# Attention output by values as the stationary operand: y comes out already turned

## The chip, the cores and the metric

The kernel runs on one core of one Trainium2 chip. The metric is the device time of one execution in microseconds (us); of several executions the median counts. TensorE (PE) multiplies and transposes, VectorE (DVE), ScalarE (ACT) and GpSimd (POOL) do elementwise work, SyncE (SP) starts transfers. SBUF is the on-chip memory, PSUM the small one into which PE writes and which POOL can't read.

## The reference

A residual stream x of 2 x 2048 tokens by 256 channels passes three parts, the first and the last of one form, with a layer norm ahead of each:

```python
x = x + 0.5 * ffn(layernorm(x))
x = x + attention(layernorm(x))
x = x + 0.5 * ffn(layernorm(x))
```

`ffn` has a shared expert of width 2048 (silu(x sg) * (x su) sd) and eight routed experts of width 1024, two per token, with a capacity. The change lies in the attention, which works on groups of 64 tokens and 16 heads of 16 channels:

```python
qkv = einsum("bglc,cd->bgld", xg, w_qkv)       # q, k: rmsnorm times ln_w
att = softmax(causal(q @ k.T / 4))             # 64 x 64 per group and head
y = att @ v
out = y.reshape(B, T, 256) @ w_proj
```

## The kernel before

Everything is float32. PE multiplies in the type float32r, so each factor is split into a high part (rounded, made by ACT) and a low part (the rest, made by DVE or POOL), and a product is three products: high by high, high by low, low by high (`split_product`, L349).

The program is one list of instructions per engine, in an order written by hand; engines wait for each other by semaphores. Its phases are: the first ffn's shared part (half of it), its experts, the **fused stage**, then the rest of the second ffn. In the fused stage (`fused_step` on each engine, 40 steps) a step runs two chunks of the shared expert (gate, up, down products of 512 tokens) and between them, for the attention, one stage each of five different tiles of 128 tokens (two groups): `stats` (layer norm), `z` (q, k, v), `keys` (scores), `probs` (softmax and values) and `out` (projection). Eight chunks make a block, so c, the chunk at which a step begins, is 0, 2, 4 or 6; with c = 0 the down product of the chunk before comes early on PE, right behind the gate product.

On PE a step with all five stages is: gate(n); two transposes of y (`y_transpose`, L505); eight transposes of the exponentials p_s (`prob_transposes`, L538); `project` (L511); q, k, v (`qkv`, L516); up(n); the down product of the chunk before; gate(n+1); transposes of q and k (`head_transposes`); `scores` (L549); up(n+1); `values` (L566); down(n); two transposes of the next tile's normed rows (`z_transpose`).

The values: ph and pl are the high and low parts of the transposed exponentials of a pair of heads, 128 keys (two groups of 64) by 128 queries. They are the stationary operand (L576, L577), vv, the v of two heads with a high and a low half, is the moving one, and y comes out as tokens by channels, in two partial columns (from v high and v low) that DVE adds up (`outputs`, L1187: a reduction per half of the rows) and multiplies by the inverse sums rden:

```python
pe.matmul(quad[:, j // 4, o:o + P], ph[:, j, :], vv[:, q, j, :, :].rearrange("p a c -> p (a c)"), start=True, stop=False)
last = pe.matmul(quad[:, j // 4, o:o + 64], pl[:, j, :], vv[:, q, j, 0, :], start=False, stop=True)
```

In the next step PE turns y_s (its channels have to lie on the partitions for the projection), ACT copies the high part yh out of PSUM (L790) and DVE forms the low part yl = y - yh, with y read from PSUM (L1225).

The row sums of the softmax are made by POOL in two halvings (`row_halves`, L1427: half_s, quarter_s), which start when ACT has written the exponentials p_s (L824); DVE adds the last 16 columns (`row_sums`, L1200) and takes the reciprocal of 16 sums a token (`inverse_sums`, L1205). In a step with c other than 0, DVE's order is: yl, stats, the addition of the projection to x, pl (L1250), qke, row sums, reciprocal, the h product (L1044), the normed q and k (L1164), the low part of v (L1156), azn, hl, qkl, the masked scores (L1179), the row maximum, the h product of n+1, the outputs, azl, hl. `scores` on PE waits for the low part of v, since it overwrites v's PSUM bank; `values` waits for the masked scores for the same reason.

Of the kernel before, what the change touches and what calls it, by code (L numbers as in the profile page):

```python
# [28 lines left out]
def program(nc, x_in, w_qkv, ln_w, w_proj, router_w, rg, ru, rd, sg, su, sd, out):  # L29
# [33 lines left out]
    with ExitStack() as ctx:  # L63
# [9 lines left out]
        def sem(name):  # L73
# [88 lines left out]
        vv = sb("vv", [P, VDEEP, NH // 2, 2, 64], F32R, att)  # L162
# [9 lines left out]
        rden = sb("rden", [P, NH], F32, att)  # L172
        y_s = sb("y_s", [P, C], F32, att)
# [3 lines left out]
        quarter_s = sb("quarter_s", [P, NH, GROUP // 4], F32, att)  # L177
# [24 lines left out]
            a_exp a_pt a_ph a_pl a_vh a_vl a_y a_yn a_yt a_yh a_yl a_o a_x a_pad a_const a_qkt a_qkh a_qkl  # L202
            qkh_sv0 qkh_sv1 qkl_sv0 qkl_sv1 heads_in0 heads_in1 a_masked a_ysum a_max a_rden a_den a_half a_quarter pool_const""".split()
# [127 lines left out]
        def wait_hl(eng, n):  # L331
            if in_fused(n):
                eng.wait_ge(sm["hl_fused"], n - FUSED[0] + 1)
            else:
                eng.wait_ge(sm["hl_done"], n + 1 - (FUSED[1] - FUSED[0] if n >= FUSED[1] else 0))

# [11 lines left out]
        def _(pe):  # L348
# [147 lines left out]
            def z_transpose(t, uses):  # L496
                pe.wait_ge(sm["a_zn"], t + 1)
                wait(pe, sm["a_pl"], t - 2)
# [39 lines left out]
            def prob_transposes(t, z, uses):  # L538
                pe.wait_ge(sm["a_exp"], t + 1)
                pe.wait_ge(sm["a_qkl"], z if z is not None else NT)  # L540
                pe.wait_ge(sm["a_zl"], z + 1 if z is not None else NT)
                if uses:
                    pe.wait_ge(sm["misc_free"], max(uses) + 1)
# [22 lines left out]
            def values(t, z, keys, out):  # L566
# [17 lines left out]
            def fused_step(s):  # L584
# [11 lines left out]
                if out is not None:  # L596
                    y_transpose(out)
# [4 lines left out]
                if probs is not None and keys is not None:  # L602
                    prob_transposes(probs, z, uses)
                if out is not None:
                    project(out)
                if z is not None:
                    qkv(z, out)
                up(n, b % 2, c, buf, SB)
# [6 lines left out]
                if keys is not None and probs is not None:  # L615
                    scores(keys, z, out)
                up(n + 1, b % 2, c + 1, buf, SB)
                if keys is not None and probs is None:
                    scores(keys, z, out)
                if any(block_at(pf, step, pb, c) is not None for step in ("T", "R", "M")):  # L620
                    wait(pe, sm["a_pl"], probs + 1 if probs is not None else upto(s, -LAG["probs"]))
# [7 lines left out]
                assert all(block_at(pf, step, pb, c + 1) is None for step in ("T", "R", "M"))  # L629
                if ahead is not None:  # L630
# [51 lines left out]
        def _(act):  # L682
# [89 lines left out]
            def values_high(t):  # L772
                act.wait_ge(sm["a_v"], t + 1)
                wait(act, sm["a_y"], t + 1 - VDEEP)
                for g in range(2):
                    for r in range(2):
                        src = quad[64 * g:64 * g + 64, 1, 0:C].rearrange("p (j r d) -> p j r d", r=2, d=HD)[:, :, r, :]
                        o = 32 * g + HD * r
                        last = nc.scalar.copy(vv[64 * r:64 * r + 64, t % VDEEP, :, 0, o:o + HD], src)
                last.then_inc(sm["a_vh"], 1)  # L780

            def fused_step(s):
# [4 lines left out]
                if out is not None:  # L787
                    act.wait_ge(sm["a_yt"], out + 1)
                    wait(act, sm["a_x"], out)
                    nc.scalar.copy(yh[:, :, :], chunks(quad[:, 1, 0:C])).then_inc(sm["a_yh"], 1)  # L790
# [13 lines left out]
                heads_first = z is not None and (c == 0 or out is None)  # L804
# [5 lines left out]
                if heads_first:  # L810
                    h_high(n, SB)
                prep(pf, pb, c)
# [42 lines left out]
        def _(dve):  # L855
# [292 lines left out]
            def values_low(t, groups=(0, 1)):  # L1148
                dve.wait_ge(sm["a_vh"], t + 1)
                q = t % VDEEP  # L1150
                for g in groups:
                    for r in range(2):
# [3 lines left out]
                        last = v.tensor_tensor(vv[rows, q, :, 1, o:o + HD], src, vv[rows, q, :, 0, o:o + HD], ALU.subtract)  # L1156
# [30 lines left out]
            def outputs(t):  # L1187
                dve.wait_ge(sm["a_y"], t + 1)
                wait(dve, sm["a_yt"], t)
# [4 lines left out]
                last.then_inc(sm["a_ysum"], 1)  # L1194
                dve.wait_ge(sm["a_rden"], t + 1)
                dve.wait_ge(sm["a_ysum"], t + 1)
                y_heads = y_s[:, :].rearrange("p (h d) -> p h d", d=HD)
                v.tensor_tensor(y_heads, y_heads, rden[:, :].unsqueeze(2).broadcast_to([P, NH, HD]), ALU.mult).then_inc(sm["a_yn"], 1)

            def row_sums(t):  # L1200
                dve.wait_ge(sm["a_quarter"], t + 1)
                wait(dve, sm["a_rden"], t)
                v.tensor_reduce(den_a[:, :], quarter_s[:, :, :], AX, ALU.add).then_inc(sm["a_den"], 1)

            def inverse_sums(t):  # L1205
                dve.wait_ge(sm["a_den"], t + 1)
                wait(dve, sm["a_yn"], t)
                v.reciprocal(rden[:, :], den_a[:, :]).then_inc(sm["a_rden"], 1)
# [10 lines left out]
            def fused_step(s):  # L1219
# [21 lines left out]
                if drained:  # L1241
                    h_product(n, SB)
                if s:
# [4 lines left out]
                if probs is not None:  # L1248
                    dve.wait_ge(sm["a_ph"], probs + 1)
# [530 lines left out]
```

## Time and profile before

| | |
|---|---|
| median of 3 runs | 2122.65 us (2120.07 to 2126.28) |
| the profiled execution | 2113.96 us |
| its span, first to last instruction | 2112.2 us |
| mean granted clock of TensorE | 0.996 of 2.4 GHz |
| busy: PE, DVE, ACT, POOL | 99%, 64%, 46%, 23% of the span |
| values products of the fused stage (L576), first and last start | 732.2 and 1269.3 us after the span's start |

The span is the time between the profile's first and last instruction; the execution's own time is 1.8 us longer. A busy PE is not PE at its peak: the ends of matmuls are modelled, and starts are the better measure of what one costs.

### The profile page before, as it was taken

The page shows a single profiled execution, that of the slowest core. Times are in us where ns is not written, and L with a number is a line of the kernel's source. Part 1 is how long each engine was busy: PE and PEld are TensorE (multiplying, and loading weights), DVE is VectorE, ACT ScalarE, POOL GpSimd, SP SyncE. Part 2 cuts the span into 40 slices and gives each one's busy share as a digit, 9 for nine tenths or more (in the row PEclk, how much of TensorE's full clock was granted, in tenths as well). Part 3 has the DMA queues.
Part 4 walks back from the last instruction along what each step waited for, and adds up shares of the span by engine and source line. Part 5 has one row for each costly group of instructions (what it writes and reads, how often), then busy time and mean ns, then how long its engine had stood idle before and what let it go on. Part 6 is the DMA issues. An engine that isn't in the chain of part 4 may idle for free.

```text
span 2112.2 us, 37639 instructions
## 1 busy us (share of the span) xinstructions
PE 2082.5 (99%) x13844; PEld 1912.4 (91%) x13844; DVE 1360.0 (64%) x3108; ACT 962.3 (46%) x1910; POOL 493.1 (23%) x433
## 2 busy tenths in 40 slices
PE   9999999999999999999999999999999999999999
PEld 7888899999998788888887888888999999988888
DVE  7666556666665688888888876665566666633333
ACT  3333335555553565655665542333455555523232
POOL 2423211121212233223334433322021211200000
PEclk9999999999999999999999999999999999999999
DMA  9331225554436344444455432221244444531010
GB/s 275 104 115 59 76 64 132 134 141 113 106 86 198 81 118 112 111 118 98 113 116 131 121 109 75 79 90 48 82 106 111 103 102 104 125 115 60 30 61 21
DMA packets 295976, 218.70 MB, mean 104 GB/s; under 512 B 69241, under 2 KB 276525, under 8 KB 295792
## 3 DMA queue, kind: packets, MB, share of 16 engines
q1 hardware_dynamic: 278128, 194.92, 32.9%
q0 software_dynamic: 17664, 21.38, 5.7%
q8 instruction: 110, 1.80, 0.4%
q14 instruction: 74, 0.61, 0.1%
HBM read 129.48 MB, written 93.23 MB: 105 GB/s over the span
## 4 chain that ended last, share of the span: by engine, by line
PE 89%; DVE 6%; issue 2%; ACT 1%; DMA 1%; SPq 1%; POOL 0%; DVEq 0%; ACTq 0%
PE gate_up_p L353 29%; PE quad L353 25%; PE out_p L391 22%; PE misc L391 4%; PE quad L576 2%; PE quad L561 2%; PE misc L545 1%; PE quad L577 1%; PE misc L417 1%; DVE h_s L1044 1%; PE misc L428 1%; PE misc L426 1%; PE misc L409 1%; DMA stage<-in_L_ffn_rd 1%; DVE p_s L1179 1%
## 5 line engine op out<-in xcount | busy, mean ns | idle before, releaser
L353 PE MATMUL gate_up_p<-zh,w 128*128 128x512 f32 (+2 forms) x2368 | 703.1, 359 | 2.0 <-DVE h_s L1044 1.4
L731 ACT CAST hh<-h_s 128x512 fp32r<-128x512 f32 (+2 forms) x511 | 276.2, 541 | 671.1 <-DVE h_s L1044 654.3
L353 PE MATMUL quad<-zh,w 128*128 128x512 f32 (+2 forms) x1728 | 481.7, 346 | 0.0
L353 PEld LDWEIGHTS gate_up_p<-zh,w 128*128 128x128 f32 x2368 | 429.9, 189 | 49.8 <-DVE h_s L1044 2.4
L391 PE MATMUL out_p<-w,hh 128*128 128x256 f32 x2808 | 458.8, 282 | 6.6 <-DVE hl L1128 5.2
L391 PEld LDWEIGHTS out_p<-w,hh 128*128 128x128 f32 x2808 | 403.8, 189 | 28.9 <-DVE hl L1128 9.0
L353 PE MATMUL gate_up_p<-zl,w 128*128 128x512 f32 (+2 forms) x1184 | 421.4, 356 | 0.0
L1044 DVE TENSOR_TENSOR h_s<-gate_up_p,sg_s 128x512 f32<-128x512 f32 (+2 forms) x296 | 178.4, 603 | 246.6 <-PE gate_up_p L353 244.6
L1060 DVE TENSOR_TENSOR hl<-h_s,hh 128x512 fp32r<-128x512 f32 (+2 forms) x431 | 247.1, 573 | 136.4 <-ACT hh L731 120.9
L353 PEld LDWEIGHTS quad<-zh,w 128*128 128x128 f32 x1728 | 308.5, 188 | 24.6
L353 PE MATMUL quad<-zl,w 128*128 128x512 f32 (+2 forms) x864 | 295.4, 342 | 0.0
L1496 POOL DMA_INDIRECT y_d<-eo,tmeta x80 | 128.8, 1611 | 617.7 <-DVE eo L943 590.2
L720 ACT ACTIVATE sg_s<-gate_up_p 128x512 f32<-128x512 f32 (+2 forms) x296 | 156.6, 529 | 212.2 <-PE gate_up_p L353 210.7
L1044 DVE TENSOR_TENSOR h_s<-quad,sg_s 128x512 f32<-128x512 f32 (+2 forms) x215 | 122.9, 572 | 200.6 <-PE quad L353 172.6
L353 PEld LDWEIGHTS gate_up_p<-zl,w 128*128 128x128 f32 x1184 | 223.5, 189 | 19.9
L391 PE MATMUL out_p<-w,hl 128*128 128x256 f32 x1404 | 225.2, 279 | 0.0
L391 PEld LDWEIGHTS out_p<-w,hl 128*128 128x128 f32 x1404 | 192.7, 189 | 0.0
L1473 POOL DMA_INDIRECT slots_d<-zn,slot_i x128 | 129.2, 1010 | 187.9 <-DVE zn L1037 143.6
L353 PEld LDWEIGHTS quad<-zl,w 128*128 128x128 f32 x864 | 162.7, 188 | 11.4
L720 ACT ACTIVATE sg_s<-quad 128x512 f32<-128x512 f32 (+2 forms) x216 | 108.7, 503 | 114.3 <-PE quad L353 113.3
L714 ACT CAST w<-stage 128x384 fp32r<-128x384 f32 x256 | 131.1, 512 | 25.7 <-DMA stage<-in_L_ffn_rd 21.9
L966 DVE TENSOR_TENSOR w<-stage,w 128x384 fp32r<-128x384 f32 x256 | 140.5, 549 | 0.0
(189 smaller groups left out, 2532.8 us busy)
## 6 DMA issues: line engine op xcount, KB each, us to landing
stage<-in_L_ffn_rg SPq DMA_DIRECT2D x128, 128.0 KB, 2.8
stage<-in_L_ffn_ru SPq DMA_DIRECT2D x128, 128.0 KB, 3.0
stage<-in_L_ffn_rd SPq DMA_DIRECT2D x128, 128.0 KB, 3.2
heads_d<-qkh SPq DMA_DIRECT2D x128, 128.0 KB
q_t<-heads_d SPq DMA_DIRECT2D x32, 384.0 KB, 4.6
k_t<-heads_d SPq DMA_DIRECT2D x64, 192.0 KB, 4.8
slots_d<-empty SPq DMA_DIRECT2D x16, 662.5 KB, 7.4
zh_d<-zh SPq DMA_DIRECT2D x16, 512.0 KB, 3.2
```

Of the source, the lines that this page charges most:

```text
L353: last = pe.matmul(dst, a, b, start=(k == 0), stop=(k == 3 * n - 1))
L391: last = pe.matmul(out[:, j // 2, o:o + C], a[:, par, cols], w[:, hi, :], start=(c == 0 and i == 0 and j % 2 == 0), stop=(c == NCH - 1 and ...
L561: last = pe.matmul(quad[0:rows, j // 4, o:o + P].rearrange("p (r c) -> p r c", r=2), queries[:, at:at + rows], k_t[:, j, :, own], start=(g ...
L576: pe.matmul(quad[:, j // 4, o:o + P], ph[:, j, :], vv[:, q, j, :, :].rearrange("p a c -> p (a c)"), start=True, stop=False)
L714: nc.scalar.copy(W[buf_of(f, u)][:, 0, j, o:o + HALF_PIECE], stage[:, j % 2, o:o + HALF_PIECE]).then_inc(sm["wh_done" if o else "wh_half"], 1)
L720: nc.scalar.activation(sg_s[:, n % 2, 0:ncol], gate_p[bank_of(n)][:, 0:ncol], ACT.Silu).then_inc(sm["silu_done"], 1)
L731: nc.scalar.copy(hh[:, n % 2, 0:ncol], h_s[:, n % 2, 0:ncol]).then_inc(sm["hh_done"], 1)
L966: last = v.tensor_tensor(w[:, 1, j, cols], stage[:, j % 2, cols], w[:, 0, j, cols], ALU.subtract)
L1044: v.tensor_tensor(h_s[:, n % 2, 0:ncol], up_p[bank_of(n)][:, 0:ncol], sg_s[:, n % 2, 0:ncol], ALU.mult).then_inc(sm["h_done"], 1)
L1060: v.tensor_tensor(hl[:, n % 2, 0:ncol], h_s[:, n % 2, 0:ncol], hh[:, n % 2, 0:ncol], ALU.subtract).then_inc(sm["hl_done"], 1)
L1473: g.indirect_dma_start(out=slots_d[f], out_offset=bass.IndirectOffsetOnAxis(ap=slot_i[:, c, t:t + 1], axis=0), in_=zn[:, k % 2, j, :], in_ ...
L1496: g.indirect_dma_start(out=y_d[f], out_offset=bass.IndirectOffsetOnAxis(ap=tmeta[:, q, j:j + 1], axis=0), in_=eo[:, par, j, :], in_offset= ...
```

## The change

The roles in the values product are exchanged. Per head pair there are now three products with 66 columns of v as the stationary operand (64 are used: two groups by two heads by 16 channels) and ph or pl as the moving one: v high by p high, v high by p low, v low by p high. y comes out with channels on the partitions and tokens along the row, as the projection needs it. So:

- the two transposes of y on PE go; the inverse sums, which lie with tokens on the partitions, are turned instead: the reciprocal writes each of the 16 values of a token 16 times (rden is 128 x 256), PE transposes it twice behind the scores (`inverse_transposes`), and ACT copies the result to rdt in SBUF;
- `outputs` on DVE is now eight products of 32 partitions by 128 elements, each picking a group's own quarter of PSUM and multiplying it by rdt; no reduction is left;
- yh and yl are formed from y_s in SBUF;
- vv has one flat row of 16 x 64 + 4 columns; quarter_s goes, the second halving writes into half_s;
- row sums and reciprocal stand in front of the low part of v in all steps (behind qkl with c = 0 before), and the drained steps at the end have an order of their own;
- POOL subtracts the low part of the weight pieces (four steps only) before its softmax subtraction, no longer behind it.

```diff
-        vv = sb("vv", [P, VDEEP, NH // 2, 2, 64], F32R, att)
+        vv = sb("vv", [P, VDEEP, NH * 64 + 4], F32R, att)
...
-        rden = sb("rden", [P, NH], F32, att)
+        rden = sb("rden", [P, NH, HD], F32, att)
+        rdt = sb("rdt", [P, KC, P], F32, att)
...
-            def y_transpose(t):
-                pe.wait_ge(sm["a_yn"], t + 1)
+            def inverse_transposes(t):
+                pe.wait_ge(sm["a_rden"], t + 1)
+                pe.wait_ge(sm["a_pl"], t + 1)
                 for k in range(KC):
-                    last = pe.transpose(quad[:, 1, k * P:(k + 1) * P], y_s[:, k * P:(k + 1) * P], ident[:, :])
-                last.then_inc(sm["a_yt"], 1)
+                    o = C + k * P
+                    last = pe.transpose(misc[:, 1, o:o + P], rden[:, NH // KC * k:NH // KC * (k + 1), :].rearrange("p h d -> p (h d)"), ident[:, :])
+                last.then_inc(sm["a_rt"], 1)
...
-                    pe.matmul(quad[:, j // 4, o:o + P], ph[:, j, :], vv[:, q, j, :, :].rearrange("p a c -> p (a c)"), start=True, stop=False)
-                    last = pe.matmul(quad[:, j // 4, o:o + 64], pl[:, j, :], vv[:, q, j, 0, :], start=False, stop=True)
+                    dst = quad[0:GROUP + 2, j // 4, o:o + P]
+                    vh, vl = (vv[:, q, (2 * j + a) * 64:(2 * j + a) * 64 + GROUP + 2] for a in range(2))
+                    pe.matmul(dst, vh, ph[:, j, :], start=True, stop=False)
+                    pe.matmul(dst, vh, pl[:, j, :], start=False, stop=False)
+                    last = pe.matmul(dst, vl, ph[:, j, :], start=False, stop=True)
...
-                    nc.scalar.copy(yh[:, :, :], chunks(quad[:, 1, 0:C])).then_inc(sm["a_yh"], 1)
+                    nc.scalar.copy(yh[:, :, :], y_s[:, :, :]).then_inc(sm["a_yh"], 1)
...
+                if probs is not None:
+                    act.wait_ge(sm["a_rt"], probs + 1)
+                    wait(act, sm["a_yn"], probs)
+                    nc.scalar.copy(rdt[:, :, :], chunks(misc[:, 1, C:2 * C])).then_inc(sm["a_rr"], 1)
...
-                yp = quad[:, :, :].rearrange("p b (j a c) -> p (b j) c a", a=2, c=64)
                 for g in range(2):
-                    rows = slice(64 * g, 64 * g + 64)
-                    last = v.tensor_reduce(y_s[rows, :].rearrange("p (j c) -> p j c", c=2 * HD), yp[rows, :, 32 * g:32 * g + 32, :], AX, ALU.add)
...
-                v.tensor_tensor(y_heads, y_heads, rden[:, :].unsqueeze(2).broadcast_to([P, NH, HD]), ALU.mult).then_inc(sm["a_yn"], 1)
+                    tokens = slice(GROUP * g, GROUP * g + GROUP)
+                    for m in range(4):
+                        rows = slice(32 * m, 32 * m + 32)
+                        own = quad[32 * g:32 * g + 32, :, m * P + GROUP * g:m * P + GROUP * g + GROUP]
+                        last = v.tensor_tensor(y_s[rows, :, tokens], own, rdt[rows, :, tokens], ALU.mult)
+                last.then_inc(sm["a_yn"], 1)
...
-                v.reciprocal(rden[:, :], den_a[:, :]).then_inc(sm["a_rden"], 1)
+                v.reciprocal(rden[:, :, :], den_a[:, :].unsqueeze(2).broadcast_to([P, NH, HD])).then_inc(sm["a_rden"], 1)
...
-                    v.tensor_tensor(yl[:, :, :], chunks(quad[:, 1, 0:C]), yh[:, :, :], ALU.subtract).then_inc(sm["a_yl"], 1)
+                    v.tensor_tensor(yl[:, :, :], y_s[:, :, :], yh[:, :, :], ALU.subtract).then_inc(sm["a_yl"], 1)
...
-                if probs is not None and c:
+                if probs is not None and not drained:
                     row_sums(probs)
                     inverse_sums(probs)
...
+                if 0 <= refill(s) < NCH:
+                    pool.wait_ge(sm["a_qkl"], z + 1)
+                    piece_low(refill(s))
                 if keys is not None:
                     pool.wait_ge(sm["a_max"], keys + 1)
                     g.tensor_tensor(p_s[:, :, :], p_s[:, :, :],
                                     smax[:, :].unsqueeze(2).broadcast_to([P, NH, GROUP]), ALU.subtract).then_inc(sm["a_sub"], 1)
-                if 0 <= refill(s) < NCH:
-                    piece_low(refill(s))
-
```

How the instructions stand, at three places. The first is PE, from the last scores product to the values; before:

```order
L561 MATMUL quad<-k_t,q_t 66x128
L353 MATMUL gate_up_p<-zh,w 128x512
L353 MATMUL gate_up_p<-zl,w 128x512
L353 MATMUL gate_up_p<-zh,w 128x512 x2
L353 MATMUL gate_up_p<-zl,w 128x512
L353 MATMUL gate_up_p<-zh,w 128x512
L576 MATMUL quad<-vv,ph 128x128
L577 MATMUL quad<-vv,pl 128x64
```

And now (L567 the scores, L513 the inverse sums' transposes, L356 the up product, L584 to L586 the values):

```order
L567 MATMUL quad<-k_t,q_t 66x128
L513 MATMUL misc<-ident,rden 128x128 x2
L356 MATMUL gate_up_p<-zh,w 128x512
L356 MATMUL gate_up_p<-zl,w 128x512
L356 MATMUL gate_up_p<-zh,w 128x512 x2
L356 MATMUL gate_up_p<-zl,w 128x512
L356 MATMUL gate_up_p<-zh,w 128x512
L584 MATMUL quad<-ph,vv 66x128
L585 MATMUL quad<-pl,vv 66x128
L586 MATMUL quad<-ph,vv 66x128
```

Two transposes have come between scores and up product, and a pair of values products has become three, with an output of 66 rows.

The second is DVE in a step with c = 0, from qke to the masked scores; before:

```order
L1254 TENSOR_SCALAR qke<-ssq 128x2
L1156 TENSOR_TENSOR vv<-quad,vv 64x8x16 x2
L1164 SCALAR_TENSOR_TENSOR qk<-quad,qkr,lnw 128x256 x2
L1156 TENSOR_TENSOR vv<-quad,vv 64x8x16 x2
L1044 TENSOR_TENSOR h_s<-gate_up_p,sg_s 128x512
L1146 TENSOR_SCALAR azn<-x,amv,ard 128x256
L1172 TENSOR_TENSOR qkl<-misc,qkh 128x512
L1203 TENSOR_REDUCE den_a<-quarter_s 128x16
L1208 RECIPROCAL rden<-den_a 128x16
L1179 TENSOR_TENSOR p_s<-quad,causal 128x1024
```

And now:

```order
L1279 TENSOR_SCALAR qke<-ssq 128x2
L1221 TENSOR_REDUCE den_a<-half_s 128x16
L1226 RECIPROCAL rden<-den_a 128x256
L1171 TENSOR_TENSOR vv<-quad,vv 64x8x16 x2
L1179 SCALAR_TENSOR_TENSOR qk<-quad,qkr,lnw 128x256 x2
L1171 TENSOR_TENSOR vv<-quad,vv 64x8x16 x2
L1059 TENSOR_TENSOR h_s<-gate_up_p,sg_s 128x512
L1161 TENSOR_SCALAR azn<-x,amv,ard 128x256
L1187 TENSOR_TENSOR qkl<-misc,qkh 128x512
```

Row sums and reciprocal have moved from behind qkl to in front of vv, and the reciprocal has grown from 16 to 256 columns.

The third is DVE from the outputs to yl, at the seam of two steps; before:

```order
L1193 TENSOR_REDUCE y_s<-quad 64x256 x2
L1198 TENSOR_TENSOR y_s<-y_s,rden 128x256
L1293 TENSOR_TENSOR azl<-misc,azh 128x256
L1128 TENSOR_TENSOR hl<-h_s,hh 128x512
L1225 TENSOR_TENSOR yl<-quad,yh 128x256
```

And now:

```order
L1211 TENSOR_TENSOR y_s<-quad,rdt 32x2x64 x8
L1315 TENSOR_TENSOR azl<-misc,azh 128x256
L1143 TENSOR_TENSOR hl<-h_s,hh 128x512
L1243 TENSOR_TENSOR yl<-y_s,yh 128x256
L948 SCALAR_TENSOR_TENSOR x<-out_p,x 128x1024
```

Two reductions and a multiplication have become eight small products, and yl reads y_s in place of quad.

## Rows read from the trace of the kernel before

**Rows 1.** The page's part 1: busy us (share of the span) and instructions.

```profile
PE 2082.5 (99%) x13844; PEld 1912.4 (91%) x13844; DVE 1360.0 (64%) x3108; ACT 962.3 (46%) x1910; POOL 493.1 (23%) x433
```

**Rows 2.** Waits of PE from 732 to 1266 us: total, times, longest.

```profile
PE quad L576 <- DVE p_s L1179: 3.3, 8, 1.3
```

**Rows 3.** PE's timeline in a step with c = 2: start us, us, instruction.

```profile
884.56 0.72 PE L391 MATMUL out_p<-w,hh 128*128 128x256 f32 x4
...
887.63 0.38 PE L508 MATMUL quad<-ident,y_s 128*128 128x128 f32 x2
887.85 1.07 PE L545 MATMUL misc<-ident,p_s 128*128 128x128 f32 x8
888.93 0.50 PE L353 MATMUL quad<-aw,yh 128*128 128x256 f32 x2
...
896.35 1.58 PE L561 MATMUL quad<-k_t,q_t 96*128 96x128 f32 x16
897.76 0.44 PE L353 MATMUL gate_up_p<-zh,w 128*128 128x512 f32 x1
...
899.24 0.33 PE L576 MATMUL quad<-vv,ph 128*128 128x128 f32 x1
...
901.05 0.72 PE L391 MATMUL out_p<-w,hh 128*128 128x256 f32 x4
```

**Rows 4.** PE's timeline in the step before it, c = 0.

```profile
867.39 0.71 PE L391 MATMUL out_p<-w,hh 128*128 128x256 f32 x4
...
870.75 0.74 PE L391 MATMUL out_p<-w,hh 128*128 128x256 f32 x4
...
873.03 0.48 PE L353 MATMUL quad<-aw,yh 128*128 128x256 f32 x2
...
879.50 1.56 PE L561 MATMUL quad<-k_t,q_t 96*128 96x128 f32 x16
...
882.75 0.33 PE L576 MATMUL quad<-vv,ph 128*128 128x128 f32 x1 [0.24 <-DVE p_s L1179]
```

**Rows 5.** VectorE's timeline in these two steps.

```profile
876.30 0.17 DVE L1254 TENSOR_SCALAR qke<-ssq 128x2 f32<-128x2 f32 x1
877.25 0.58 DVE L1156 TENSOR_TENSOR vv<-quad,vv 64x128 fp32r<-64x128 f32 x2 [0.79 <-ACT vv L779]
...
888.46 0.42 DVE L1225 TENSOR_TENSOR yl<-quad,yh 128x256 fp32r<-128x256 f32 x1 [0.55 <-ACT yh L790]
...
891.27 1.23 DVE L1250 TENSOR_TENSOR pl<-misc,ph 128x1024 fp32r<-128x1024 f32 x1 [0.90 <-ACT ph L795]
...
892.93 0.25 DVE L1208 RECIPROCAL rden<-den_a 128x16 f32<-128x16 f32 x1
893.49 0.69 DVE L1044 TENSOR_TENSOR h_s<-gate_up_p,sg_s 128x512 f32<-128x512 f32 x1 [0.31 <-PE gate_up_p L353]
...
894.88 1.19 DVE L1156 TENSOR_TENSOR vv<-quad,vv 64x128 fp32r<-64x128 f32 x4
```

**Rows 6.** ScalarE's timeline in the step of rows 3.

```profile
886.71 1.06 ACT L824 ACTIVATE p_s<-p_s 128x1024 f32<-128x1024 f32 x1
888.05 0.37 ACT L790 CAST yh<-quad 128x256 fp32r<-128x256 f32 x1 [0.28 <-PE quad L508]
...
901.07 0.62 ACT L731 CAST hh<-h_s 128x512 fp32r<-128x512 f32 x1 [2.29 <-DVE h_s L1044]
```

**Rows 7.** Timeline of POOL and VectorE in a later step.

```profile
1165.94 1.28 POOL L1429 TENSOR_TENSOR half_s<-p_s 128x512 f32<-128x512 f32 x1 [0.61 <-ACT p_s L824]
1165.99 1.78 DVE L1128 TENSOR_TENSOR hl<-h_s,hh 128x512 fp32r<-128x512 f32 x1
```

**Rows 8.** VectorE's groups by shape, whole run: busy us, mean ns | idle before.

```profile
L1193 DVE TENSOR_REDUCE y_s<-quad 64x256 f32<-64x512 f32 x64 | 43.9, 687 | 10.6 <-PE quad L577 10.2
...
L1208 DVE RECIPROCAL rden<-den_a 128x16 f32<-128x16 f32 x32 | 8.1, 253 | 1.1
...
L890 DVE RECIPROCAL rec<-vare 128x4 f32<-128x4 f32 x15 | 2.7, 178 | 0.5
```

More of the change, by code:

```diff
@@ L335, in wait_hl, with vv_at @@
                 eng.wait_ge(sm["hl_done"], n + 1 - (FUSED[1] - FUSED[0] if n >= FUSED[1] else 0))
+        def vv_at(rows, q, part):
+            return vv[rows, q, 0:NH * 64].rearrange("p (j a c) -> p j a c", a=2, c=64)[:, :, part, :]
         def tile_at(s, stage):
@@ L601, in fused_step @@
                     down_of(*chunk_before(f, phase, b, c))
-                if probs is not None and keys is not None:
+                if out is not None and keys is not None:
                     prob_transposes(probs, z, uses)
@@ L607, in fused_step @@
                     qkv(z, out)
+                if probs is not None and out is None:
+                    prob_transposes(probs, z, uses)
                 up(n, b % 2, c, buf, SB)
@@ L616, in fused_step @@
                     scores(keys, z, out)
+                if probs is not None:
+                    inverse_transposes(probs)
                 up(n + 1, b % 2, c + 1, buf, SB)
-                if keys is not None and probs is None:
-                    scores(keys, z, out)
                 if any(block_at(pf, step, pb, c) is not None for step in ("T", "R", "M")):
-                    wait(pe, sm["a_pl"], probs + 1 if probs is not None else upto(s, -LAG["probs"]))
+                    wait(pe, sm["a_rr"], probs + 1 if probs is not None else upto(s, -LAG["probs"]))
                     wait(pe, sm["a_qkl"], upto(s, 1 - LAG["z"]))
@@ L629, in fused_step @@
                 assert all(block_at(pf, step, pb, c + 1) is None for step in ("T", "R", "M"))
+                if keys is not None and probs is None:
+                    scores(keys, z, out)
                 if ahead is not None:
@@ L803, in fused_step @@
                     values_high(z)
-                heads_first = z is not None and (c == 0 or out is None)
+                heads_first = z is not None and c == 0
                 if not heads_first:
@@ L1242, in fused_step @@
                     h_product(n, SB)
+                    if probs is not None:
+                        prob_low(probs)
+                    fused_low(n)
+                    if probs is not None:
+                        row_sums(probs)
+                        inverse_sums(probs)
+                    if keys is not None:
+                        masked(keys)
                 if s:
@@ L1254, in fused_step @@
                     v.tensor_scalar(qke[:, :], ssq[:, :], 1.0 / C, RMS_EPS, ALU.mult, ALU.add).then_inc(sm["a_qke"], 1)
-                if probs is not None and c:
+                if probs is not None and not drained:
                     row_sums(probs)
                     inverse_sums(probs)
-                heads_first = z is not None and (c == 0 or out is None)
+                heads_first = z is not None and c == 0
                 if not heads_first and not drained:
@@ L1270, in fused_step @@
                     normal(ahead)
-                if not heads_first:
+                if not heads_first and not drained:
                     fused_low(n)
@@ L1274, in fused_step @@
                     heads_low(z)
-                if probs is not None and not c:
-                    row_sums(probs)
-                    inverse_sums(probs)
                 if keys is not None and probs is None:
                     h_product(n + 1, SB)
-                if keys is not None:
+                if keys is not None and not drained:
                     masked(keys)
@@ L1436, in fused_step @@
                 f, phase, b, c = fused_chunk(s)
-                z, keys, probs, ahead = (tile_at(s, stage) for stage in ("z", "keys", "probs", "stats"))
+                z, keys, probs, out, ahead = (tile_at(s, stage) for stage in ("z", "keys", "probs", "out", "stats"))
                 n = chunk(f, phase, b, c)
```

43 lines of the change are left out of this document (20 added, 23 removed).

## The prediction

> **What bounds the kernel now.** I read the engines' busy time first: TensorE (PE) is busy for 2082.5 of the span's 2112.2 us [rows 1], so only what lengthens or shortens PE's own sequence, or makes PE wait, moves the end. The change touches no transfer, and of the work the fused stage alone (attention between shared-expert chunks, 32 token tiles in 40 steps). The list of waits, cut to the steps that hold values, shows how little PE waits there: its longest sum is 3.3 us in 8 waits, for the masked scores [rows 2]. Then I followed one step through the engines' timelines. I call V the moment when a step's last values product is issued and the down product behind it starts. Three steps in four (those in which c is 2, 4 or 6) run as [rows 3] do, from V = 884.56 to the next V at 901.05, 16.49 us; the step with c = 0 [rows 4] runs from 867.39 to 884.56, 17.17 us. All times below are us after V.
>
> What sets the pace in [rows 3] is nearly even. PE's probability transposes start at 3.29, 0.08 after ScalarE's exponential ends (886.71 + 1.06, 3.21) [rows 6]. The projection starts at 4.37, when VectorE has formed y's low part (3.90 + 0.42) [rows 5]. The scores start at 11.79, 0.28 after VectorE's last low part of v (894.88 + 1.19, 11.51) [rows 5]. VectorE is thus off the end only by some tenths of a us: the reader should see in [rows 5] that it waits just 0.31 before its h product, behind the reciprocal.
>
> **The change, part by part, in a step with c other than 0.**
>
> *Values on PE.* Now 16 products, each with a stationary operand 128 wide, take 1.81 (899.24 to 901.05), 0.113 each [rows 3]. They become 24 with a stationary operand 66 wide and 128 moving columns. The scores are eight of each width in 1.41 (896.35 to 897.76) [rows 3]; less 8 times 0.113, a 66-wide one costs 0.063. I take 24 x 0.063 = 1.51, a gain of 0.30. Bounds: 0.058 (0.113 x 66/128) and 0.113, that is 1.39 to 2.71. By the Trainium skill, "TensorE: Matmul & The Clock Gate", Back-to-back issue gap, a stream of loads and products of 128 columns holds about 81 ns each; by it the values would take an estimated 1.94, a loss of 0.13 in place of the gain. No row here shows 81 ns at that width.
>
> *Transposes.* The two of y leave the start of the step (0.22, 887.63 to 887.85 [rows 3]); but the probability transposes still need the exponential, so they start at about 3.27 as before. Two of the inverse sums enter between scores and up product; they cost 0.15 (bounds 0.13 and 0.22). They wait for the reciprocal, which ends long before the scores do, so the up product queued behind them is not held. ScalarE's copy of them (as yh, 0.37) falls into its idle time before hh, 2.29 [rows 6].
>
> *Outputs on VectorE.* Two reductions of 0.69 [rows 8] and a multiplication end 1.92 after they start. Now come eight products of 32 partitions by 128 elements. The nearest row is the low part of v, 64 x 128, four in 1.19 [rows 5], 0.30 each: 8 x 0.30 = 2.4, +0.5. Bounds 0.21 and 0.42 each (half and the whole of yl's 256 elements [rows 5]). Behind them azl and hl end at about 3.68 in place of 3.3.
>
> *y's low part.* It read PSUM and SBUF; now y_s and yh both lie in SBUF. [Rows 7] show what that means while GpSimd (POOL) adds the row halves: an SBUF-with-SBUF subtraction issued at 1165.99, just after POOL's 1.28, lasts 1.78: it ends 0.55 after POOL does. The old yl, of the same step place but from PSUM, is not held: 0.42, inside POOL's time [rows 5]. POOL starts at the exponential's end, and yh comes behind the exponential on ScalarE, so yl is always issued inside POOL's 1.28. With hl in front of it holding POOL up a little, POOL's 1.28 runs from about 3.5 to 4.75; yl has half the elements of the held row, so it ends 0.29 behind POOL, at 5.04, and the projection starts at 5.10 (0.05 after yl, as 888.93 is after 888.88): 0.73 later than now. The row sums that POOL also delays have 3 us to spare.
>
> *The reciprocal.* 16 elements become 256. Another operation on 256, yl, costs 0.42 [rows 5]; this one costs 178 ns on 4 and 253 on 16 [rows 8], 6.25 ns an element, so 0.253 + 240 x 0.00625 = 1.75. Bounds 0.42 (the rate of other rows) and 4.0 (16 rows of 16). I take the slope, since it comes from the operation itself. The Trainium skill, "VectorE: DVE Perf Modes", First, the fixed hardware budget, calls it an iterative divide repeated 8 times; at the 0.96 GHz of its Specifications that is 8.3 ns an element and an estimated 2.25 us, some 15 us more in all than the sum below. The rows show the lower slope.
>
> *The path.* Behind the projection come the q and k product and ScalarE's squares of it; VectorE's qke, which needs them, starts 3.27 after the projection (873.03 [rows 4] to 876.30 [rows 5]): 8.37. The row sums start 0.07 later and take 0.45, so the reciprocal starts at 8.89 and h at 8.89 + 1.67 = 10.56 (two operations in a row overlap by 0.08). Now h starts at 8.93 [rows 5]. From h to the scores VectorE's sequence is unchanged, 2.58 to the end of v's low part and 0.06 more: scores at 13.20. PE alone would be there at 5.10 + 7.42 (888.93 to 896.35 [rows 3]) = 12.52, so a new wait in front of the scores, for the low part of v, sets the step. Scores to values takes 2.89 + 0.15, the values 1.51: V at 17.75. **+1.26.**
>
> **The step with c = 0.** The down product that now starts at 3.36 (870.75 [rows 4]) needs hl, which ends at 3.68: +0.38. The collision of yl is covered by that product. Row sums and reciprocal come in front of the low part of v, where VectorE now waits 0.79 for ScalarE [rows 5]: qke starts at 8.91 + 0.38, the sums at 9.36, and the reciprocal ends at 11.48; v's low part, at 9.86 now, starts then. The scores come 2.25 after v's first low part (877.25 to 879.50 [rows 4, 5]), at 13.73, against 12.11. From scores to values it is 3.25, of which the wait of 0.24 for the masked scores [rows 4] goes, since the sums no longer stand in front of them; with 0.15 and 1.51, V comes at 18.40. **+1.23.**
>
> **The sum.** 15 steps x 1.26 = 18.9; 6 x 1.23 = 7.4; the eight later steps that also carry routing or weight pieces, where VectorE is fuller: 1.3 each, 10.4, less 4 for the weight pieces that POOL now subtracts before its softmax subtraction, clear of hl and yl ([rows 7] are such a case of crowding). First and drained steps: 0, within 2. Together +32.7 us. The profiled execution took 2113.96; the median of the three timed runs is 2122.65 (2120.07 to 2126.28), above it by 8.7. Against the median I forecast 2155; against the profiled execution it would be 2146. About 0.3% (6.4 us) is what a measurement of this kernel can tell from no change.
>
> **Rivals.**
> - *yl gets through before POOL* (its neighbour hl holds the access until just before). Then the projection starts behind the eight transposes, near 4.15. yh starts at 3.11 instead of 3.49, so pl comes at 6.33 instead of 6.71 [rows 5, 6], the reciprocal 1.66 later at 7.99, h at 9.66, V at 16.85: +0.36 in 15 steps, 5.4; 7.4; eight at 0.7 less 4, 1.6. +14, 2137. Against it: in [rows 7] the vector operation waits for POOL's end.
> - *The reciprocal costs 0.42*, as other 256-element rows, with yl held. Then h waits for up, 4.56 after the projection (888.93 to 893.49), 9.66; scores at 12.52, V at 17.07: +0.58 in 15 steps, 8.7; c = 0: 0; the rest 0. +9, 2132. Against it: the slope of its own two rows.
> - *The other side: VectorE's additions fit into its idle time and PE goes on setting the step.* Place: the stretch from yl to the h product. It decides where the reciprocal stays below about 0.8 us and yl is not held: then up bounds h (4.15 + 4.56), scores start at 4.15 + 7.42 less 0.1 of restart, V at 16.02, -0.47 in 15 steps, 7.0; c = 0: 0; the rest -6. -13, 2110. For it: PE's own sequence does get shorter by the values' 0.30. Against it: both rows named above.
> - *The narrow stationary operand saves nothing*: 0.113 each, values 2.71, which adds 1.20 in 29 steps to the forecast: 2190. Against it: the scores' rows.
>
> **How the numbers follow.** Forecast 0.50; yl free 0.15; cheap reciprocal 0.16; the other side 0.12; wide price 0.07. The cheap reciprocal lies at the bound, half of it counts as the same. Faster 0.12, same 0.08, slower 0.80. The forecast's own range is 2143 to 2168 (outputs, loaded steps). The range reaches down over two rivals and up for dearer outputs, leaving out the last two rivals: 2128 to 2170.
>
> **What would show it.** Right: a reciprocal near 1.75; yl near 1.3 to 1.5 instead of 0.42; PE's longest wait in the stage in front of the scores, for the low part of v, about 0.7 in three steps of four; values in 1.5; steps of 17.7 and 18.4. Wrong: a reciprocal below 0.8, or scores that start within 0.3 of the q and k transposes' end in steps that are not longer than 16.5.

## The result and the profile after

The changed kernel takes 2185.51 us, the median of 4 runs (2183.81 to 2187.58); the kernel before took 2121.38 beside it. The ratio is 1.0295, with a 95% interval of 1.0276 to 1.0314. The forecast was 2155, from 2128 to 2170: slower, as it said, but by 64 us in place of 33.

The two profiled executions lie 71.5 us apart in span (2183.7 against 2112.2). The page's part 1 after, against [rows 1]:

```profile
PE 2097.1 (96%) x14100; PEld 1914.0 (88%) x14100; DVE 1444.9 (66%) x3268; ACT 971.5 (44%) x1942; POOL 498.7 (23%) x433
```

VectorE (DVE) has 85 us more to do, and TensorE (PE) waits. The list of PE's waits from 700 to 1345 us (what is waited for: total, times, longest):

```profile
PE misc L540 <- DVE qk L1179: 22.5, 18, 3.1
PE quad L356 <- DVE yl L1243: 17.1, 21, 1.3
PE quad L567 <- DVE vv L1171: 10.8, 21, 0.5
PE out_p L394 <- DVE hl L1143: 8.4, 11, 3.5
PE misc L513 <- DVE rden L1226: 5.3, 2, 3.3
```

In the kernel before, the same stretch has for the first four of these places:

```profile
PE out_p L391 <- DVE hl L1128: 5.2, 4, 1.9
...
PE misc L535 <- DVE qk L1164: 2.4, 4, 1.2
PE quad L561 <- DVE vv L1156: 2.0, 4, 0.5
...
PE quad L353 <- DVE yl L1225: 1.5, 3, 0.8
```

The second and third after are the two that were forecast (y's low part, v's low part). The first, q and k transposes that wait for VectorE's normalized q and k, which stand behind the reciprocal, was not named in the forecast: 7.2 us of it lie in the regular steps (1.1 in each with c = 0), 11.7 behind them.

**Most regular steps with c not 0 are as forecast.** Nine of the 15 take 17.69 to 17.73 us (forecast 17.75). PE's timeline of one of them, with c = 4, from V = 925.72 to the next V at 943.41, 17.69 us (the step just before it, the one that answers to [rows 3], took 19.00 and comes further down):

```profile
925.72 0.68 PE L394 MATMUL out_p<-w,hh 128*128 128x256 f32 x4
...
928.98 1.06 PE L551 MATMUL misc<-ident,p_s 128*128 128x128 f32 x8
930.79 0.50 PE L356 MATMUL quad<-aw,yh 128*128 128x256 f32 x2 [0.74 <-DVE yl L1243]
...
938.90 1.57 PE L567 MATMUL quad<-k_t,q_t 96*128 96x128 f32 x16 [0.51 <-DVE vv L1171]
940.31 0.40 PE L513 MATMUL misc<-ident,rden 128*128 128x128 f32 x2
...
941.94 0.22 PE L584 MATMUL quad<-ph,vv 128*66 128x128 f32 x1
942.00 0.23 PE L585 MATMUL quad<-pl,vv 128*66 128x128 f32 x1
942.06 0.22 PE L586 MATMUL quad<-ph,vv 128*66 128x128 f32 x1
```

The projection starts at V + 5.07 (forecast 5.10), the scores at V + 13.18 (13.20), and the values follow each other at 0.06 us. VectorE and POOL in the same step, against [rows 5] and [rows 7]:

```profile
929.24 1.49 DVE L1243 TENSOR_TENSOR yl<-y_s,yh 128x256 fp32r<-128x256 f32 x1
...
934.04 0.17 DVE L1279 TENSOR_SCALAR qke<-ssq 128x2 f32<-128x2 f32 x1 [0.71 <-ACT qk L812]
934.12 0.42 DVE L1221 TENSOR_REDUCE den_a<-half_s 128x16 f32<-128x256 f32 x1
934.58 1.75 DVE L1226 RECIPROCAL rden<-den_a 128x256 f32<-128x256 f32 x1
936.24 0.63 DVE L1059 TENSOR_TENSOR h_s<-gate_up_p,sg_s 128x512 f32<-128x512 f32 x1
...
937.57 1.19 DVE L1171 TENSOR_TENSOR vv<-quad,vv 64x128 fp32r<-64x128 f32 x4
```

```profile
928.96 1.49 POOL L1452 TENSOR_TENSOR half_s<-p_s 128x512 f32<-128x512 f32 x1 [1.67 <-ACT p_s L839]
```

y's low part starts while POOL adds and ends 0.28 after it; the reciprocal takes 1.75; h starts at V + 10.52 (10.56).

**What was not forecast is elsewhere.** Measured between the starts of the down product behind the values, the two traces compare so (us in the profile of before, and what the others have more or less; the experiments' columns come into use below). The eight loaded steps carry routing or weight pieces besides what the regular ones do; the two drained ones, at the end, no longer have the q, k, v stage:

| | before | after | recip16 | yl_first | both | scalar_copy_filled |
|---|---|---|---|---|---|---|
| up to the first values' end | 734.0 | +9.7 | +4.7 | +8.0 | +4.5 | +0.1 |
| 15 regular steps, c not 0 | 247.4 | +23.0 | +12.1 | +7.5 | -4.5 | -5.0 |
| 6 regular steps, c = 0 | 103.1 | +8.6 | -1.2 | +10.2 | -1.1 | -1.6 |
| 8 loaded steps | 151.4 | +22.4 | +6.7 | +23.5 | +5.7 | -1.3 |
| 2 drained steps | 33.8 | +5.8 | +5.1 | +5.4 | +1.3 | -0.3 |
| the rest | 842.4 | +2.0 | +1.2 | +1.5 | +3.1 | +0.4 |
| span | 2112.2 | +71.5 | +28.5 | +56.1 | +9.1 | -7.7 |

The forecast had 18.9, 7.4, 6.4 and 0 for the lines from regular to loaded and the others together. And TensorE's granted clock fell: its mean is 0.986 after and 0.996 before. The windows of two equal steps with c = 0, one without and one with a fall, two stretches inside the latter, and a loaded step (from and to, length, busy us of PE, PEld, DVE, ACT, POOL with instructions, granted clock, DMA share, GB/s):

```profile
888.64:906.72 18.08, 16.46 (x126) 14.20 (x124) 16.93 (x34) 10.58 (x21) 5.12 (x5) 1.00 0.56 141
815.84:835.51 19.67, 18.05 (x126) 15.43 (x124) 17.73 (x34) 11.12 (x22) 6.45 (x6) 0.91 0.52 146
...
831.00:832.00 1.00, 1.00 (x6) 0.90 (x5) 0.83 (x1) 0.37 (x1) 0.00 (x0) 0.50 0.35 86
832.00:833.00 1.00, 1.00 (x4) 0.80 (x3) 1.00 (x3) 0.99 (x1) 0.00 (x0) 0.50 0.53 181
...
1190.35:1213.61 23.26, 19.78 (x127) 17.27 (x126) 18.71 (x45) 12.03 (x23) 10.83 (x9) 0.85 0.42 104
```

PE's work is the same 126 instructions, but takes 18.05 us in place of 16.46, since the clock stands at 0.50 (1.2 GHz) in stretches such as the two shown. Over the span 1 - 0.986 of 2183.7 is 30.6 us, against 8.4 before. By this estimate some 22 of the 71.5 us are clock, and 49 are work and waits; it counts PE as if it set the pace throughout the stretches at 0.50, so 22 is rather too much than too little. About 10 of the 22 lie in the loaded steps (granted clock 0.92 over their 173.8 us, 0.98 over the 151.4 before).

### The profile page after: what moved, and what is told of

It reads as the page before. It is cut to its first block, busy times and chain, and to the rows that moved or that the text cites. A ratio compares the mean times of both kernels' runs of the same rounds, so it can differ in the third digit from the quotient of the medians.

```text
span 2183.7 us, 38401 instructions
## 1 busy us (share of the span) xinstructions
PE 2097.1 (96%) x14100; PEld 1914.0 (88%) x14100; DVE 1444.9 (66%) x3268; ACT 971.5 (44%) x1942; POOL 498.7 (23%) x433
## 4 chain that ended last, share of the span: by engine, by line
PE 47%; DVE 15%; issue 5%; ACT 1%; DVEq 0%; POOL 0%; ACTq 0%; POOLq 0%
PE quad L356 15%; PE gate_up_p L356 14%; PE out_p L394 11%; DVE y_s L1211 3%; PE misc L394 2%; DVE hl L1143 2%; PE quad L567 2%; DVE h_s L1059 1%; DVE yl L1243 1%; DVE qk L1179 1%; DVE vv L1171 1%; DVE p_s L1194 1%; DVE rden L1226 1%; DVE pl L1216 1%; DVE den_a L1221 1%
## 5 line engine op out<-in xcount | busy, mean ns | idle before, releaser
L356 PE MATMUL gate_up_p<-zh,w 128*128 128x512 f32 (+2 forms) x2368 | 710.6, 362 | 1.0 <-DVE zl L1373 0.5
L356 PE MATMUL quad<-zh,w 128*128 128x512 f32 (+2 forms) x1728 | 481.8, 346 | 0.0
L356 PEld LDWEIGHTS gate_up_p<-zh,w 128*128 128x128 f32 x2368 | 433.2, 190 | 51.2 <-issue 1.9
L356 PE MATMUL gate_up_p<-zl,w 128*128 128x512 f32 (+2 forms) x1184 | 424.6, 359 | 0.2 <-issue 0.2
L356 PEld LDWEIGHTS quad<-zh,w 128*128 128x128 f32 x1728 | 308.5, 188 | 24.7
L356 PE MATMUL quad<-zl,w 128*128 128x512 f32 (+2 forms) x864 | 295.4, 342 | 0.0
L356 PEld LDWEIGHTS gate_up_p<-zl,w 128*128 128x128 f32 x1184 | 225.2, 190 | 19.8
L356 PEld LDWEIGHTS quad<-zl,w 128*128 128x128 f32 x864 | 162.7, 188 | 11.4
L725 ACT CAST w<-stage 128x384 fp32r<-128x384 f32 x256 | 131.1, 512 | 25.3 <-DMA stage<-in_L_ffn_rd 22.3
```

What stands on the lines that cost most here:

```text
L356: last = pe.matmul(dst, a, b, start=(k == 0), stop=(k == 3 * n - 1))
L725: nc.scalar.copy(W[buf_of(f, u)][:, 0, j, o:o + HALF_PIECE], stage[:, j % 2, o:o + HALF_PIECE]).then_inc(sm["wh_done" if o else "wh_half"], 1)
```

## Experiments

Theory A: the wide reciprocal and the held low part of y lengthen VectorE's chain, and the waits that they give PE also let its clock fall. Theory B: what exceeds the forecast comes from the moved orders in the filling steps (those ahead of the first values), the loaded and the drained ones. Each ratio below is to the kernel before as timed beside that run; its median went from 2116.02 to 2121.38 us, so differences between runs are given by the ratios too.

**recip16**: the reciprocal of 16 sums, then a copy 16 times wide.

```diff
+rd_a = sb("rd_a", [P, NH], F32, att)
...
-v.reciprocal(rden[:, :, :], den_a[:, :].unsqueeze(2).broadcast_to([P, NH, HD])).then_inc(sm["a_rden"], 1)
+v.reciprocal(rd_a[:, :], den_a[:, :]).then_inc(sm["a_ra"], 1)
+dve.wait_ge(sm["a_ra"], t + 1)
+v.tensor_copy(rden[:, :, :], rd_a[:, :].unsqueeze(2).broadcast_to([P, NH, HD])).then_inc(sm["a_rden"], 1)
```

> The changed kernel, but the reciprocal is taken of 16 sums and then copied 16 times wide by VectorE (about 0.25 + 0.35 us in place of 1.75). Theory A (the wide reciprocal and the held low part of y lengthen VectorE's chain, and TensorE's waits that follow also let its granted clock fall): every step loses about 1.1 us and most of the stretches at a granted clock of 0.5 go; 2130 to 2150 us. Theory B (the loss beyond the forecast comes from the moved orders, in the filling, loaded and drained steps): only the regular steps gain, 21 x 0.7 = 15 us; 2165 to 2175 us, mean clock still near 0.986.

Measured: 2142.48, ratio 1.0114 (1.0098 to 1.0131), mean clock 0.994. VectorE's groups (busy us, mean ns):

```profile
L1229 DVE COPY rden<-rd_a 128x256 f32<-128x256 f32 x32 | 9.4, 294 | 1.1
L1227 DVE RECIPROCAL rd_a<-den_a 128x16 f32<-128x16 f32 x32 | 8.1, 253 | 1.1
```

1753 ns have become 547 (253 + 294), and 43 us go (38 by the two ratios): theory A. The table has 10.9 of them in the regular steps with c not 0, 9.8 in those with c = 0, and 22.3 in the other lines.

**yl_first**: POOL's row halves wait until y's low part is formed.

```diff
 pool.wait_ge(sm["a_exp"], t + 1)
+wait(pool, sm["a_yl"], t)
```

> The changed kernel, but GpSimd's row halves wait until the low part of y is formed. Theory A: the low part of y takes 0.4 to 0.5 us in place of 1.26, the projection starts 0.8 us earlier, steps with c other than 0 get 0.7 us shorter, some falls of the clock go; 2155 to 2170 us. Theory B: 2180 to 2190 us, since other work is late by as much.

Measured: 2170.09, ratio 1.0246 (1.0229 to 1.0263). Timeline of a step with c not 0 (16.8 us long):

```profile
936.81 0.42 DVE L1243 TENSOR_TENSOR yl<-y_s,yh 128x256 fp32r<-128x256 f32 x1
937.36 1.28 POOL L1453 TENSOR_TENSOR half_s<-p_s 128x512 f32<-128x512 f32 x1 [2.53 <-ACT p_s L839]
```

The price of the collision is shown: 15 us between the two profiles (10 by the ratios), and the steps with c not 0 hold it (23.0 to 7.5). That some falls of the clock would go was wrong: the mean clock is 0.984, no higher than without the edit.

**both**: both edits.

> Both edits together (16-wide reciprocal with a copy; row halves behind the low part of y). Theory A: TensorE's own sequence sets most steps again, with the values 0.3 us shorter; 2110 to 2130 us, mean granted clock 0.993 or more. Theory B: 2145 to 2165 us, mean clock still near 0.986.

Measured: 2123.32, ratio 1.0018 (1.0004 to 1.0031), clock 0.993. So 59 of the 63 us (by the ratios) were these two prices together with the falls behind them, more than the 38 and 10 of the single edits added. Nine of the 15 regular steps with c not 0 now take 16.0 to 16.1 against 16.5: PE's timeline has no wait in them, and its sequence is shorter. Those with c = 2 take 16.3 to 16.4, and one takes 17.0.

**before_recip256**: the kernel before with the wide reciprocal, nothing else.

```diff
-rden = sb("rden", [P, NH], F32, att)
+rden = sb("rden", [P, NH, HD], F32, att)
...
-v.reciprocal(rden[:, :], den_a[:, :]).then_inc(sm["a_rden"], 1)
+v.reciprocal(rden[:, :, :], den_a[:, :].unsqueeze(2).broadcast_to([P, NH, HD])).then_inc(sm["a_rden"], 1)
```

> The kernel before, but its reciprocal writes all 256 elements (1.75 us in place of 0.25) and the product with y reads them; nothing else is changed. Theory A: the scores come 1.2 us later in 15 steps and in most loaded ones, and waits of that length bring falls of the clock; 2145 to 2165 us. Theory B: at most 21 x 0.7 us; 2125 to 2140 us, mean clock still 0.995 or 0.996.

Measured: 2172.41, ratio 1.0260 (1.0231 to 1.0290), clock 0.986. This is above both theories' ranges: the falls are there, as theory A has it, but it priced the whole too low. Windows of two steps, c = 2 and c = 4, columns as above:

```profile
897.85:917.48 19.63, 19.05 (x117) 16.60 (x116) 14.84 (x27) 9.66 (x20) 4.70 (x6) 0.88 0.30 68
917.48:934.86 17.38, 16.83 (x117) 14.54 (x116) 14.83 (x27) 10.11 (x20) 5.13 (x6) 1.00 0.38 92
```

One operation that is 1.5 us longer in each of 32 steps, 48 us in all, costs the kernel before 54 us (2172.41 less 2118.62). The undisturbed step grew by 0.9 (16.49 to 17.38), the one with a fall by 3.1. (1 - 0.986) of 2167.7 is 30.3 us of clock, 22 more than before. By the same estimate 32 us would be left without the clock's part.

**wait_filled**: the changed kernel with PE's longest waits filled.

```diff
-def gate(n, z, c, buf, ncol):
+def gate(n, z, c, buf, ncol, again=0):
     w = W[buf]
     wait(pe, sm["silu_done"], bank_before(n) + 1)
+    for _ in range(again):
+        pe.matmul(gate_p[bank_of(n)][:, 0:ncol], w[:, 0, c, 0:P], zh[:, z, 0, 0:ncol], start=True, stop=True)
...
-gate(n + 1, b % 2, c + 1, buf, SB)
+gate(n + 1, b % 2, c + 1, buf, SB, 4 if z is not None and (c == 0 or s >= 29) else 0)
```

> The changed kernel, but in the steps in which TensorE waits 1 us and more for the normalized q and k (those with c = 0, and from step 29 on), the gate product ahead of that wait is begun by four more products of 512 columns whose result is overwritten: 0.92 us of work in place of waiting, in 15 steps. Theory A (the falls of the granted clock follow TensorE's long waits): fewer stretches at 0.5, mean clock 0.989 or more, 2168 to 2180 us, although TensorE has 14 us more to do. Theory B (the falls have nothing to do with these waits): mean clock still 0.986, 2183 to 2197 us.

Measured: 2179.14 (2178.16 to 2186.63), ratio 1.0289 (1.0260 to 1.0317); its four runs have clocks of 0.993, 0.994, 0.989 and 0.992, those of the changed kernel 0.986 to 0.989. (There were 14 such steps, not 15: 56 products, some 13 us.) The mean clock is as theory A has it, and the median too, but the time can't be told from that of the changed kernel, though PE has 13 us more to do. The step that showed a fall above, in this run:

```profile
814.65:832.75 18.10, 17.42 (x130) 14.99 (x128) 16.97 (x34) 10.57 (x21) 5.14 (x5) 1.00 0.54 142
```

18.10 in place of 19.67, with four more products: the fall is gone, and so is the second one of its kind (19.65 to 18.06). Over the loaded steps the granted clock is 0.97 in place of 0.92. One step that was not filled, with c = 2, now shows a fall: 20.54 us at a clock of 0.92, in place of 19.00 at 1.00. So for the clock theory A is borne out in the main: most of the falls go when PE's waits are filled. Which of several equal steps falls, the waits inside it don't tell: the two in the first windows above have the same two waits, 0.48 and 1.07. That stays open.

**both_ends**: both edits, the scores of the filling step as before the change, and row sums and reciprocal ahead of the h product in the drained steps.

```diff
 up(n + 1, b % 2, c + 1, buf, SB)
+if keys is not None and probs is None:
+    scores(keys, z, out)
...
 if drained:
+    if probs is not None:
+        row_sums(probs)
+        inverse_sums(probs)
     h_product(n, SB)
...
```

> As the run with both edits, and besides: the scores of the filling step stand in front of the weight preparation and the down product, as before the change, and in the drained steps row sums and reciprocal come in front of the h product. Theory A (what the orders cost after both edits is in the filling and the drained steps): the 3.5 us wait for h's low part falls to 2, the wait of the inverse transposes (2.9 us in two steps) goes; 2113 to 2119 us. Theory B (it is in the loaded steps, where VectorE is full): 2120 to 2124 us.

Measured: 2126.08 (2119.17 to 2132.57), ratio 1.0028 (1.0013 to 1.0044): above both theories' ranges, and no gain over both. In the profile, taken of one of the faster runs (2121.00), the wait for h's low part fell to 2.0 and the drained steps got 2.5 us shorter, but the loaded steps stayed at +5.7, which is theory B's place.

**both_pool**: both edits, and POOL's weight pieces again behind its softmax subtraction.

```diff
-if 0 <= refill(s) < NCH:
-    pool.wait_ge(sm["a_qkl"], z + 1)
-    piece_low(refill(s))
 if keys is not None:
...
+if 0 <= refill(s) < NCH:
+    piece_low(refill(s))
```

> As the run with both edits, but GpSimd subtracts the weight pieces behind the softmax's subtraction again, as before the change. Theory A (the new order of the pieces helps by about 4 us in the loaded steps, as forecast): 2125 to 2129 us. Theory B (with the pieces first, the exponential is late, and the probability transposes wait for it up to 2.3 us): 2117 to 2121 us.

Measured: 2127.30, ratio 1.0034 (1.0020 to 1.0049), whose interval meets that of both. The median lies in theory A's range, 4 us above that of both, but not by the loaded steps, where the pieces are: they take 156.5 against 157.1 in the two profiles, and what the profile has more lies in the filling and drained steps. So the gain of 4 us that the forecast credited to the new order is not shown.

**scalar_copy**: as both_ends, but ScalarE makes the wide copy, ahead of h's high part, and in the drained steps the inverse transposes stand behind the up product.

```diff
...
+act.wait_ge(sm["a_ra"], probs + 1)
+wait(act, sm["a_rt"], probs)
+nc.scalar.copy(rden[:, :, :], rd_a[:, :].unsqueeze(2).broadcast_to([P, NH, HD])).then_inc(sm["a_rden"], 1)
...
```

> As the run with both edits and both ends, but ScalarE makes the 16-wide copy of the reciprocals (0.29 us off VectorE in every step), and in the drained steps the inverse transposes stand behind the up product. Theory A (VectorE's fullness sets the loaded steps): their 5.7 us over before become 3 or less, regular steps stay at 16.0 and 17.0; 2114 to 2120 us. Theory B (they are set by waits that this does not touch, or ScalarE's copy makes h's high part late by 0.4 us): loaded steps as they were, 2121 to 2127 us.

Measured: 2113.79, ratio 0.9974 (0.9965 to 0.9984), just under theory A's range. The loaded steps, which the second change does not touch, stand at +2.1 in place of +5.7: 0.29 us off VectorE in each was worth 0.45. By the Trainium skill, "Perfetto Trace Analysis", Optimizing Scalar/DVE Operations, work that either engine can do may go to Scalar where VectorE is full; here that agrees in the loaded steps, although the copy itself takes 405 ns there against 294 on VectorE:

```profile
L821 ACT COPY rden<-rd_a 128x256 f32<-128x256 f32 x32 | 13.0, 405 | 16.8 <-DVE rd_a L1233 16.3
```

**scalar_copy_filled**: that, with the repeated gate products of wait_filled in steps 31, 32, 35 and 36 alone.

> As the run with ScalarE's copy, and in the four steps where TensorE still waits over 1 us for the normalized q and k (31, 32, 35 and 36) four more products of 512 columns, overwritten afterwards, stand in that wait. Theory A (the falls of the clock follow those waits): the falls in these steps go, mean clock 0.996 or more, 2110 to 2116 us. Theory B: the added 3.7 us show, 2120 to 2128 us.

Measured: 2108.90 (2106.19 to 2111.88), ratio 0.9960 (0.9946 to 0.9974), a little below theory A's range and the lowest ratio of all the runs. The clock of its profile:

```profile
core 0: 2104.5 us, clock 0.998
```

Its interval meets that of scalar_copy, so what the filling adds there is not settled.

**before_filled**: the control, the kernel before with the same filling.

> A control: the kernel before, with the same four more products in steps 31, 32, 35 and 36 and nothing else. Theory A (the gain of the last kernel comes from the shorter values, about 6.6 us in the regular steps, and filling brings the kernel before little, since its waits are shorter): 2114 to 2122 us. Theory B (the gain is the filling's alone): 2106 to 2111 us, as the last kernel.

Measured: 2121.70, ratio 1.0026 (1.0016 to 1.0037). The filling alone does not make the kernel before faster, rather 0.26% slower (only 2.0 of the 9.8 us that its profile has more lie in the loaded steps, where the products stand); the last kernel's gain is not the filling's alone. Its regular steps carry it (-5.0 and -1.6 in the table).

## Why the prediction was right and wrong

- *Values*: 24 at 0.06 are 1.47 us (forecast 1.51), right. By the 81 ns of the Trainium skill, "TensorE: Matmul & The Clock Gate", Back-to-back issue gap, which the prediction weighed, they would have taken an estimated 1.94; the trace does not bear that out at this width.
- *Outputs, reciprocal, y's low part*: the groups of the whole run (busy us, mean ns) are these; forecast were 300, 1750, and 1300 to 1500 in three steps of four.

```profile
L1211 DVE TENSOR_TENSOR y_s<-quad,rdt 32x128 f32<-32x128 f32 x256 | 72.3, 282 | 13.8 <-PE quad L586 10.5
L1226 DVE RECIPROCAL rden<-den_a 128x256 f32<-128x256 f32 x32 | 56.1, 1753 | 1.1
L1243 DVE TENSOR_TENSOR yl<-y_s,yh 128x256 fp32r<-128x256 f32 x32 | 40.4, 1263 | 3.5 <-ACT yh L801 3.5
```

  The slope of the two short reciprocals [rows 8], 6.25 ns an element, held up to 256. The 2.25 us that the prediction estimated from the Trainium skill, "VectorE: DVE Perf Modes", First, the fixed hardware budget, are not what the trace shows. Where y's low part ends, V + 5.01 against 5.04, is partly luck: POOL was not held up by hl as the prediction had it, but started on time, at V + 3.24, and took 1.49 in place of 1.28.
- *The path with c not 0*: 17.69 against 17.75 in nine of 15, right, though PE's longest wait there is the one for y's low part (0.74), not the one in front of the scores (0.51), which the prediction had named as a sign. The sum of the 15 is 23.0 against 18.9. Four of the steps with c = 2, right behind one with c = 0, take 18.1 to 19.0, and the last two of the 15 take 18.2 and 18.5, with a wait for q and k. In the four, outputs start 0.57 to 0.59 after V in place of 0.20, and in three of them a second collision was missed: hl, not only yl, meets POOL (1.77 to 1.79 in place of 0.68). VectorE, POOL and PE in the one from V = 906.72, which answers to [rows 3]:

```profile
907.30 2.35 DVE L1211 TENSOR_TENSOR y_s<-quad,rdt 32x128 f32<-32x128 f32 x8
...
910.03 1.79 DVE L1143 TENSOR_TENSOR hl<-h_s,hh 128x512 fp32r<-128x512 f32 x1
911.74 0.95 DVE L1243 TENSOR_TENSOR yl<-y_s,yh 128x256 fp32r<-128x256 f32 x1
```

```profile
910.01 1.26 POOL L1452 TENSOR_TENSOR half_s<-p_s 128x512 f32<-128x512 f32 x1 [1.23 <-ACT p_s L839]
911.35 1.06 POOL L1454 TENSOR_TENSOR half_s<-half_s 128x256 f32<-128x256 f32 x1
```

```profile
910.37 1.06 PE L551 MATMUL misc<-ident,p_s 128*128 128x128 f32 x8 [0.41 <-DVE azl L1315]
912.75 0.50 PE L356 MATMUL quad<-aw,yh 128*128 128x256 f32 x2 [1.31 <-DVE yl L1243]
```

- *c = 0*: 18.1 against 18.40 in four of six, with PE's wait (1.07) at the transposes of q and k and not in front of the scores; two took 19.66, with a fall of the clock.
- *The term that failed* is the line "First and drained steps: 0, within 2" with "the eight later steps ... 1.3 each, 10.4, less 4". They measured 17.5 and 22.4 in place of 0 and 6.4 (2.1 of the 17.5 lie ahead of the stage, whose first transposes start anywhere from 688.5 to 693.8 us in the twelve profiles, whatever the kernel). The prediction said itself that VectorE is fuller in the loaded steps, and then priced them like the others. They grew by 2.8 us each, the regular ones by 1.5, with waits for q and k of up to 3.0; by the clock's estimate some 10 of their 22.4 us are clock, which leaves about 1.5 each. That this is the reciprocal's full 1.5 is not shown. But putting the reciprocal back took 22.3 us off these lines (15.7 of them in the loaded steps), where the forecast's rival with a cheap one had only 6.4 for them.
- *A term that was missing*: PE's clock. PE was taken as one engine that either works or waits; the 22 us by which the falls grew, by the estimate above, are about a third of the difference in span. The kernel before had them too, 8.4 us in a mean clock of 0.996, and the prediction read none of those stretches.
- *The rivals*: yl free was priced 18 us below the forecast (2137 against 2155), measured 10 to 15. A cheap reciprocal was 23 below, measured 38 to 43. The other side, PE setting the step, came true once both prices were gone: -0.47 a step was worked out for it, 7.0 in the 15 steps, and the run with both edits has it in nine of them and 4.5 us in all.

What is not settled: where the last 5 us between both and the kernel before come from. No run took away the outputs alone, or the new place of the row sums; undoing POOL's order alone, and two other orders together, gave no gain. What the clock costs in time is an estimate throughout: filling the waits took most falls away, but the time as a whole, with 13 us more for PE to do, stayed where it was.

## What to carry to other kernels

When an engine with little idle time gets more to do, price the added time for each kind of step by its own idle time: here the fullest steps grew by 2.8 us each and the regular ones by 1.5, under the same change. Add a term for TensorE's clock wherever new waits appear, and read the stretches at half clock that the kernel already has. A reciprocal of few values that are wanted many times over should run on the few and be copied wide, on the engine that has time; and two operations of VectorE and GpSimd on SBUF alone should be put one behind the other if TensorE waits for one of them.

## What the runs showed of the hardware

- Work that TensorE does in vain, in place of waiting, can cost nothing: 56 products of 512 columns, about 13 us, left the time where it was within its interval, with a mean clock of 0.993 in place of 0.986 in the profiled runs. The kernel before, whose waits are short, got no faster with 16 of them (ratio 1.0026).
- The granted clock fell to 0.50 in regular steps whose longest wait was only 1.07 us, and equal steps beside them kept it at 1.00.
- The copy of 16 values to 256 places took 294 ns on VectorE, where the reciprocal written so wide took 1753, though it too has only 16 different values to read: its time went by the 256 places.
- A subtraction of 256 elements with both inputs in SBUF took 420 ns in the mean when GpSimd's addition was made to wait for it, and 1263 when it was not; issued inside that addition, it ended 0.28 us behind it.
